# A recurrent loop's output products with tokens as weights, and its gates in halves by batch

## The reference

```
def step(carry, inp):
    w0_, w1_, w2_ = carry
    qi, ki, vi, lr0i, lr1i, lr2i = inp
    gate = ki @ w0_
    hb = ki @ w2_
    sg = silu(gate)
    hidden = sg * hb
    dhidden = vi @ w1_.transpose(0, 2, 1)
    dhbm = dhidden * sg
    dgate = dhidden * hb
    dgba = silu_backprop(dgate, gate)
    w1g = newtonschulz5(einsum('bch,bcd->bhd', hidden * lr1i, vi))
    w0g = newtonschulz5(einsum('bcd,bch->bdh', ki * lr0i, dgba))
    w2g = newtonschulz5(einsum('bcd,bch->bdh', ki * lr2i, dhbm))
    (each weight: w = w + wg, then its columns are scaled to their first norms)
    oi = silu(qi @ w0_) * (qi @ w2_) @ w1_
    return ((w0_, w1_, w2_), oi)
```

## Time and profile before

| | |
|---|---|
| runs | 1030.43, 1031.6, 1032.62 us, median 1031.6 |
| the profiled execution's span | 1028.6 us |
| PE / DVE / ACT / POOL busy | 970.8 / 702.0 / 564.1 / 435.5 us |
| recurrent loop | steps t = 1 to 7 from about 85 us to 363 us |
| granted TensorE clock | 0.998 of full speed over the span |

### The profile page before, as it was taken

One profiled execution on the slowest core, in us unless ns is written; L12 is line 12 of the kernel. 1 busy time (PEld: TensorE's weight loads), 2 busy tenths in 40 slices (PEclk: granted clock), 3 DMA queues, 4 the chain that ended last, 5 costly groups with the idle time before them and its releaser, 6 DMA issues.

```text
span 1028.6 us, 25039 instructions
## 1 busy us (share of the span) xinstructions
PE 970.8 (94%) x9714; PEld 737.7 (72%) x9714; DVE 702.0 (68%) x2121; ACT 564.1 (55%) x1450; POOL 435.5 (42%) x391
## 2 busy tenths in 40 slices
PE   5887999999999999999999999999999999999978
PEld 3566897887887755675656769786978687868546
DVE  4889988988989942213223676866686668776864
ACT  3667778777778732212223465555556556655541
POOL 1221240340541711101002666775677567779710
PEclk9999999999999999999999999999999999999999
DMA  9250000000000002900002321322132213211202
GB/s 313 68 195 2 2 0 0 0 0 0 0 2 2 2 1 48 308 1 0 1 1 51 84 61 44 72 63 52 43 73 63 52 43 72 58 37 45 92 2 84
DMA packets 32812, 52.36 MB, mean 51 GB/s; under 512 B 7760, under 2 KB 17744, under 8 KB 31824
## 3 DMA queue, kind: packets, MB, share of 16 engines
q1 hardware_dynamic: 32720, 51.10, 18.0%
HBM read 21.98 MB, written 2.10 MB: 23 GB/s over the span
## 4 chain that ended last, share of the span: by engine, by line
PE 54%; DVE 4%; ACT 2%; issue 1%
PE quad L2102 12%; PE quad L2061 10%; PE quad L1705 8%; PE quad L2119 7%; PE quad L2005 6%; PE quad L2133 5%; PE quad L2197 1%; PE quad L2069 1%; PE quad L1591 1%; ACT act_probs L2366 1%; PE quad L2024 1%; DVE act_probs L2457 1%; DVE wq_wo L2471 1%; DVE x_pairs L2487 0%; ACT act_probs L2357 0%
## 5 line engine op out<-in xcount | busy, mean ns | idle before, releaser
L2709 POOL TENSOR_TENSOR act_probs<-act_probs,rden 128x512 f32<-128x512 f32 (+3 forms) x128 | 169.0, 1327 | 111.1 <-DVE rden L2476 111.1
L2357 ACT ACTIVATE act_probs<-act_probs,neg_max 128x256 f32<-128x256 f32 (+3 forms) x256 | 140.9, 553 | 83.3 <-DVE neg_max L2457 83.1
L2061 PEld LDWEIGHTS quad<-hT,ug_queries 128*128 128x128 f32 x1024 | 122.6, 192 | 14.1 <-issue 7.7
L2061 PE MATMUL quad<-hT,ug_queries 128*128 128x128 f32 x1024 | 124.7, 275 | 0.8 <-DVE act_probs L1720 0.5
L2457 DVE CUSTOM_DVE_ANT_0 act_probs<-quad,mask 128x256 f32<-128x256 f32 (+3 forms) x256 | 115.1, 485 | 0.3 <-issue 0.3
L1705 PE MATMUL quad<-hT,ug_raw_switch 128*128 128x512 f32 x256 | 113.9, 595 | 0.0
L1720 DVE SCALAR_TENSOR_TENSOR act_probs<-quad,ws_up,silu_keys 128x512 f32<-128x512 f32 x32 | 24.0, 750 | 97.1 <-ACT silu_keys L1715 97.1
L1715 ACT ACTIVATE silu_keys<-quad,ws_gate 128x512 f32<-128x512 f32 x32 | 22.0, 687 | 118.7 <-PE quad L1705 118.7
L1705 PEld LDWEIGHTS quad<-hT,ug_raw_switch 128*128 128x128 f32 x256 | 47.5, 190 | 55.1 <-issue 54.3
L2476 DVE RECIPROCAL rden<-den 128x2 f32<-128x2 f32 x128 | 20.3, 159 | 94.2 <-ACT act_probs L2357 94.0
L2102 PE MATMUL quad<-down_raw_out,ug_raw_switch 128*128 128x256 f32 (+3 forms) x256 | 79.5, 438 | 3.6 <-DVE neg_max L2457 3.6
(11 more groups left out here) (330 smaller groups left out, 2285.7 us busy)
## 6 DMA issues: line engine op xcount, KB each, us to landing
rope_swapped<-gate SPq DMA_DIRECT2D x120, 64.0 KB, 2.0
ug_raw_switch<-gate SPq DMA_DIRECT2D x60, 128.0 KB, 2.3
ug_raw_switch<-in_wmod SPq DMA_DIRECT2D x4, 512.0 KB, 7.4
x_pairs<-in_x SPq DMA_DIRECT2D x4, 512.0 KB, 8.0
x_rows<-x_pairs SPq DMA_DIRECT2D x8, 256.0 KB, 5.0
wq_wo<-in_wq_nopeT SPq DMA_DIRECT2D x1, 2048.0 KB, 8.5
wq_wo<-in_wo SPq DMA_DIRECT2D x1, 2048.0 KB, 13.2
ug_queries<-in_switch_w SPq DMA_DIRECT2D x1, 2048.0 KB, 7.6
```

The lines of the kernel that those rows point to most:

```text
L2061: mm = nc.tensor.matmul(out[:, P * i:P * i + P], w[:, kt, HP * half + i, :], k.hT[:, kt, b, cols], start=(kt == 0), stop=(kt == KT - 1))
L2357: nc.scalar.activation(tile, tile, ACT.Exp, bias=neg_max[:, r, e:e + 1], scale=-1.0, accum_out=den[:, r, e:e + 1])\
L2709: nc.gpsimd.tensor_tensor(tile, tile, rden[:, t % RING, :].unsqueeze(2).to_broadcast([P, 2, cols]), ALU.mult)\
```

## The change

Two of the four output products of a step are formed for w0 and w2 at once: `out_gate(t, i)` has the 64 tokens of q as the stationary operand and 256 moving columns, as the gates have, so its result has tokens on the partitions, once for each pair. ACT takes the silu of half of bank 6 (`silu_gate`), DVE multiplies in place of `hidden_out` (`hidden_rows`), both once for each pair, and as the next product wants the hidden index on the partitions, `turn_hidden` transposes the four 128x128 blocks on PE and `take_hidden` copies them on ACT. The first pair's comes where `out_product(0, 0)` was, the second's where `out_product(1, 0)` was; the products in `early_out` and after (A, 1) are gone; the transposes stand before the turned v, and `out_rows` moves from behind (AA, 2) to behind (AA, 3). `silu_gate(t, 1)` stands ahead of the load of the Sqrt table. In place of `gates`, `gate(i, 1)` of both pairs comes first, waiting for weights 3 and 4 alone, then `gate(i, 0)` and `back(i)` of each pair; the gates lie in banks 4 and 3, `back` in banks 1 and 0. The first gradients wait for the four activations of the first pair. The tail after the loop keeps its `out_product`s. The constant for the output norm moves to the shared semaphore of constants.

```diff
-N_CONSTS = 4
+N_CONSTS = 5
...
-    PROJECT_V, TURN_OUT, TURN_V, TURN_QK, OUT_ROWS, SUMS, START = range(PH, PH + 7)
-    G_ORDER = ((GT, 0), (SUMS, 0), (OUT_ROWS, 0), (SUMS, 1), (SUMS, 2), (GT, 2), (SUMS, 3), (SUMS, 4), (GT, 4), (SUMS, 5))
+    PROJECT_V, TURN_OUT, TURN_V, TURN_QK, OUT_ROWS, SUMS, START, OUT_GATE, TURN_HID = range(PH, PH + 9)
+    GATE_BANK, DH_BANK = (4, 3), (1, 0)
+    G_ORDER = ((GT, 0), (SUMS, 0), (OUT_GATE, 1), (SUMS, 1), (SUMS, 2), (GT, 2), (SUMS, 3), (SUMS, 4), (GT, 4), (SUMS, 5))
     G_REST = (1, 3, 5)
-    INNER = ((A, 0), (A, 1), (OUT_ROWS, 1), (START, 0), (A, 2), (A, 3), (AA, 0), (A, 4), (AA, 1), (START, 1), (A, 5), (TURN_V, 0), (AA, 2), (OUT_ROWS, 0), (START, 2), (AA, 3), (Y, 0), (AA, 4), (AA, 5), (START, 3), (TURN_QK, 0), (Y, 1),
+    INNER = ((A, 0), (A, 1), (START, 0), (A, 2), (A, 3), (AA, 0), (A, 4), (AA, 1), (START, 1), (A, 5), (TURN_HID, 0), (TURN_V, 0), (AA, 2), (START, 2), (AA, 3), (OUT_ROWS, 0), (Y, 0), (AA, 4), (AA, 5), (START, 3), (TURN_QK, 0), (Y, 1),
...
-    TAKEN = ((AA, 0), (START, 0), (AA, 1), (TURN_V, 0), (START, 1), (AA, 2), (OUT_ROWS, 0), (START, 2), (TURN_QK, 0), (START, 3), (TURN_QK, 1), (TURN_OUT, 0), (START, 4), (A1, 0), (A1, 1), (A1, 2), (START, 5), (A1, 3), (A1, 4), (YT, 0), (A1, 5), (YT, 1), (TURN_OUT, 1), (YT, 2), (START, 6),
+    TAKEN = ((AA, 0), (START, 0), (AA, 1), (TURN_HID, 0), (TURN_V, 0), (START, 1), (AA, 2), (OUT_ROWS, 0), (START, 2), (TURN_QK, 0), (START, 3), (TURN_QK, 1), (TURN_OUT, 0), (START, 4), (A1, 0), (A1, 1), (A1, 2), (START, 5), (A1, 3), (A1, 4), (YT, 0), (A1, 5), (YT, 1), (TURN_OUT, 1), (YT, 2), (START, 6),
...
-            def gates(t):
-                for i in range(PAIRS):
-                    for hd in range(H):
-                        for j in range(2):
-                            mm = nc.tensor.matmul(bank[3 * i][C * j:C * j + C, 2 * HD * hd:2 * HD * hd + 2 * HD],
-                                                  kT[:, i, hd, C * j:C * j + C], weight[:, 3 * j:3 * j + 2, H * i + hd, :],
-                                                  start=True, stop=True)
+            def gate(i, j):
+                for hd in range(H):
+                    mm = nc.tensor.matmul(bank[GATE_BANK[i]][C * j:C * j + C, 2 * HD * hd:2 * HD * hd + 2 * HD],
+                                          kT[:, i, hd, C * j:C * j + C], weight[:, 3 * j:3 * j + 2, H * i + hd, :],
+                                          start=True, stop=True)
+                if j == 0:
                     mm.then_inc(s["gates_summed"], 1)
-                    for hd in range(H):
-                        for j in range(2):
-                            mm = nc.tensor.matmul(bank[3 * i + 1][C * j:C * j + C, HD * hd:HD * hd + HD],
-                                                  vT[:, i, hd, C * j:C * j + C], state[:, 3 * j + 2, H * i + hd, :],
-                                                  start=True, stop=True)
-                    mm.then_inc(s["gates_summed"], 1)
+
+            def back(i):
+                for hd in range(H):
+                    for j in range(2):
+                        mm = nc.tensor.matmul(bank[DH_BANK[i]][C * j:C * j + C, HD * hd:HD * hd + HD],
+                                              vT[:, i, hd, C * j:C * j + C], state[:, 3 * j + 2, H * i + hd, :],
+                                              start=True, stop=True)
+                mm.then_inc(s["gates_summed"], 1)
+
+            def out_gate(t, i):
+                if i == 0:
+                    pe.wait_ge(s["proj_taken"], t)
+                    pe.wait_ge(s["q_moved"], t)
+                else:
+                    pe.wait_ge(s["out_hidden"], 2 * t - 1)
+                for hd in range(H):
+                    for j in range(2):
+                        mm = nc.tensor.matmul(bank[6][C * j:C * j + C, 2 * HD * hd:2 * HD * hd + 2 * HD],
+                                              qT[:, i, hd, C * j:C * j + C], weight[:, 3 * j:3 * j + 2, H * i + hd, :],
+                                              start=True, stop=True)
+                mm.then_inc(s["out_summed"], 1)
+
+            def turn_hidden(t):
+                pe.wait_ge(s["out_hidden"], 2 * t)
+                for u in range(U):
+                    mm = nc.tensor.transpose(bank[6][:, P * u:P * u + P], h_o[:, P * u:P * u + P], k.eye[:])
+                mm.then_inc(s["o_turned"], 1)
...
             def out_rows(c, at=6):
-                pe.wait_ge(s["out_hidden"], c + 1)
+                if at == 6:
+                    pe.wait_ge(s["hid_taken"], c + 1)
+                else:
+                    pe.wait_ge(s["out_hidden"], 2 * NCH - 1)
...
-                def early_out(t):
-                    pe.wait_ge(s["proj_taken"], t)
-                    pe.wait_ge(s["q_moved"], t)
-                    begin(3, G)
-                    out_product(0, 1, 0)
-
...
-                if not first:
-                    early_out(t)
                 pe.wait_ge(s["qkv_taken"], 3 * (t + 1))
                 if first:
                     first_norm.wait_halves(pe, 3, 1)
                     pe.wait_ge(w_in, STATE_IN)
                 else:
-                    for q in (0, 1, 3, 4):
+                    for q in (3, 4):
                         begin(q, G)
-                    pe.wait_ge(s["w_scaled"], Q * t)
-                gates(t)
+                for i in range(PAIRS):
+                    gate(i, 1)
+                if not first:
+                    for q in (0, 1):
+                        begin(q, G)
+                for i in range(PAIRS):
+                    gate(i, 0)
+                    if i == 0 and not first:
+                        pe.wait_ge(s["w_scaled"], Q * t)
+                    back(i)
...
-                    begin(0, G)
-                    out_product(0, 0, 0)
+                    out_gate(t, 0)

                 pe.wait_ge(s["lr_applied"], PAIRS if first else 3 * PAIRS * (t + 1))
                 pe.wait_ge(s["dh_used"], 2 * PAIRS * (t + 1))
+                pe.wait_ge(s["gate_acted"], 4 * PAIRS * t + 4)
...
                     else:
-                        if n == 0:
-                            pe.wait_ge(s["out_silued"], t)
-                        out_product(1, n)
+                        out_gate(t, n)
...
+                    elif ph == TURN_HID and not first:
+                        turn_hidden(t)
                     elif ph == OUT_ROWS and not first:
-                        if n == 1:
-                            out_product(1, 1)
-                        else:
-                            out_rows(t - 1)
+                        out_rows(t - 1)
...
+            def silu_gate(t, i):
+                act.wait_ge(s["out_summed"], 2 * (t - 1) + i + 1)
+                nc.scalar.activation(h_o[:, H * P * i:H * P * i + H * P].rearrange("p (h d) -> p h d", h=H),
+                                     bank[6][:].rearrange("p (h g d) -> p h g d", h=H, g=2)[:, :, 0, :], ACT.Silu).then_inc(s["out_silued"], 1)
+
+            def take_hidden(t):
+                act.wait_ge(s["o_turned"], 2 * t - 1)
+                nc.scalar.activation(hid_o[:].rearrange("p i h c -> p (i h c)"), bank[6][:], ACT.Copy).then_inc(s["hid_taken"], 1)
+
...
-                act.wait_ge(s["o_turned"], c + 1)
+                act.wait_ge(s["o_turned"], 2 * c + 2 if at == 6 else 2 * c + 1)
...
-                gh = [bank[3 * i][:].rearrange("p (h g d) -> p h g d", h=H, g=2) for i in range(PAIRS)]
+                gh = [bank[GATE_BANK[i]][:].rearrange("p (h g d) -> p h g d", h=H, g=2) for i in range(PAIRS)]
...
                 if not first:
-                    silu_out(t - 1)
+                    silu_gate(t, 0)
                 for n, q in enumerate(MQ):
                     if n != G_DVE:
                         take(G, g_bf, q)
+                if not first:
+                    silu_gate(t, 1)
                 load_table(ACT.Sqrt)
...
+                    elif ph == TURN_HID and not first:
+                        take_hidden(t)
...
-            def hidden_out(c, at=6):
-                dve.wait_ge(s["out_silued"], c + 1)
+            def hidden_rows(t, i):
+                dve.wait_ge(s["out_silued"], 2 * (t - 1) + i + 1)
+                to = h_o[:, H * P * i:H * P * i + H * P].rearrange("p (h d) -> p h d", h=H)
+                nc.vector.tensor_tensor(to, bank[6][:].rearrange("p (h g d) -> p h g d", h=H, g=2)[:, :, 1, :], to, ALU.mult)\
+                    .then_inc(s["out_hidden"], 1)
+
+            def hidden_out(c, at):
+                dve.wait_ge(s["out_silued"], 2 * NCH - 1)
                 dve.wait_ge(s["out_summed"], 2 * c + 2)
                 nc.vector.tensor_tensor(hid_o[:].rearrange("p i h c -> p (i h c)"), bank[at][:], h_o[:], ALU.mult).then_inc(s["out_hidden"], 1)
...
-                dh = [bank[3 * i + 1][:, 0:D].rearrange("p (h d) -> p h d", h=H) for i in range(PAIRS)]
+                dh = [bank[DH_BANK[i]][:, 0:D].rearrange("p (h d) -> p h d", h=H) for i in range(PAIRS)]
...
                 by_silu(1)
```

(17 more changed lines are left out.)

## The result

The changed kernel takes 1040.1 us (median; 1038.4 to 1042.6) beside 1031.0 for the kernel before on the same chip (1029.3 to 1032.6): the ratio is 1.0083, with an interval of 1.0060 to 1.0105. It is slower, by about 9 us, where 7.0 were forecast. The profiled execution has a span of 1038.4 us where before has 1028.6.

A forecast was written before the change was run, and what follows sets the result against it. Each step was taken as a PE part, a mixed part and a DVE-bound part that any later start delays. 6 x 0.95 + 1.3 = 7.0 us; 1028.6 + 7.0 + 3.0 = 1038.6 us, range 1032.5 to 1041.5.

The forecast's parts named there:

- Gates in halves: PE up to the gradients: same-half instructions run in line, 15 x 0.216 = 3.24 us; stretch 4.30 against 3.78, +0.52.
- Rival 1: Gates: 64-wide instructions of one half overlap at 0.108 us each, a step ends 0.6 earlier, 1027.4 us; chance 0.08.
- Changes of width: PE switching between full-width and 64-wide instructions costs about 0.1 us each way; out_gate +0.13, so gradients start 0.65 later.
- Column sums: out_gate number 1 replaces the third output product on PE: 0.1 + 0.87 + 0.1 against 0.92, +0.15 us.
- ACT behind the table load: silu_gate number 1 ahead of the Sqrt table load uses up ACT's 0.32 us of room; 0 to 0.3 more.
- Rival 3: silu_gate ahead of the table load costs 0.3 us beyond the room each step; 1040.7 us; chance 0.14.
- Mixed part: First Newton-Schulz products: AA 4 instead of AA 3 holds DVE, 0.15 us later beyond the shift; bounds -0.5 to +0.3.
- Rival 2: Mixed part: out_rows behind AA 3 removes DVE's 0.73 us gap, giving back 0.5 a step; 1033.7 us; chance 0.18.
- the DVE part: Step from 224.10 to 244.60: DVE busy 20.32 of 20.50 us, so any later beginning lengthens the step by as much.
- Per step: Steps t = 1 to 6 each grow by 0.52 + 0.13 + 0.15 + 0.15 = 0.95 us.
- Last step: t = 7, without q/k norm on DVE: AA 4 comes 0.5 us later in place of 0.15, so 1.3 us in all.
- A step of 40 us, and 6.3 us to the gradient: Signs of being right: 40 us steps; last turned weight to first gradient 6.3 us where it was 5.65.

The follow-up runs named there:

- after_pool_held: The changed kernel with one wait more: in the last step POOL's copy of q waits for DVE's four normalisations; 1033.4 us, ratio 1.0021.
- before_pool_early: The kernel before with the last step's fourth output product moved up behind the third, releasing POOL early; 1038.0 us, ratio 1.0062.
- after_all_j1_then_j0: The changed kernel with POOL held in the last step, all weights awaited, then eight j = 1 gates, eight j = 0, then d_hidden; 1038.3 us, ratio 1.0077.

## Why the prediction was right in the whole and wrong in its parts

The direction held, and the time, 1040.1, is 1.5 above the forecast and inside its range. But that is luck: two errors of 4.1 and 4.8 us cancel. Of the 8.6 to 9.1 us that the runs show, 7.65 are there at the landmark behind the loop; the rest is put down to nothing here.

- **Gates in halves, +0.52 a step: wrong, -0.17.** The term "only the first of j = 0 runs beside the last of j = 1" failed. Four do, which is 0.65 us off the 4.30; 3.64 were measured. The pairs of rows 5 gave the right price of two in line and of two side by side; what they could not show is how far ahead a half is taken, and I put the lowest value into the sum. Rival 1 is out: instructions of one half stay 0.216 apart, not 0.108. What was gained came from the other half's starting early.
- **Changes of width, 0.1 each: right.** The transposes ahead of out_gate take 1.02 where 0.93 stood, and out_gate takes 1.01 with the change behind it (0.97 forecast). Together +0.16 where +0.13 stood. So the gradients, due 0.65 later, are 0.0 later.
- **Column sums, +0.15: right** (+0.17).
- **ACT behind the table load, 0 to 0.3, taken 0: a little low.** g_norm starts without any wait for PE, 0.55 behind g_total's product where it was 0.44 (217.16 to 217.71; 216.50 to 216.94): 0.11. Rival 3 is there in kind, with a third of its price. The turned gradients, which set the pace of the next products, come 0.17 later (218.15 - 0.49 against 217.49), so this 0.11 did not add to the column sums' 0.17.
- **Mixed part, +0.15: about right** (+0.08: 0.25 at the second polynomial, 0.17 at the column sums). The gap moved from AA 3 to AA 4 and is 1.11 where "about 1" was forecast. Rival 2, that DVE profits, is out, and the kernels with out_rows later say why: PE is as full as DVE there, and DVE's wait comes back ahead of a later product. That the DVE part is bound by DVE alone, as the first paragraph of the prediction has it, was too simple.
- **Per step:** 0.17 + 0.08 = 0.25 in the step of the rows; 0.29 between the mean steps of the table, 1.6 us for t = 1 to 6 by the landmark of the column sums, where 5.7 stood.
- **Last step, +1.3: wrong, 6.1** (7.65 at the landmark, less 1.6). Without the meeting (after_pool_held) the products do bring DVE to the state updates about 1 us late (352.92 against 351.01 before, of which 0.9 was there in the column sums), but at the next ones the two kernels are together again (357.77 and 357.62), and the last step is 0.5 us shorter than before's (44.33 and 44.83), so even the 1.3 went. The meeting puts 6.4 to 6.7 us on top. The prediction moved the second product ahead and looked only at those who wait for it in the loop. For the last step it counted PE and DVE; that POOL waits for both products before it moves q was not followed, though before's POOL row at 336.58 waits 8.79 us for PE. That is the step that failed: a released engine was costed at nothing, and it met DVE.
- **A step of 40 us, and 6.3 us to the gradient: wrong** (39.5, and 5.67). These two signs alone, read in the trace, would have told that the sum was right by luck.

What stays open: why an instruction starts up to four places ahead and no further, and what the 2.8 us at the lower clock cost by themselves in the last step; POOL's release was not tried without PE's pause.

## What to carry to other kernels

When a change moves a product earlier, list every engine that waits for its semaphore, in the first and last step too, and look what each does once released: an engine that starts earlier can slow another that it used to miss. Here 2.8 us earlier on an idle engine cost 6.4 us (before_pool_early). A wait that keeps such an engine off a short critical operation is cheap: one line gave back 6.4 of the 8.6 us. And where two engines are both full, moving work between places of one moves the other's wait and can make it longer; time the order, don't argue it from one gap.

## What the runs showed of the hardware that was not expected

- TensorE started 64-wide instructions ahead of others that stood before them in the program: L567 at 210.50 before L558 at 210.71 in after_all_j1_then_j0. By the spacing of the starts one column half passed three instructions of the other (206.697 and 206.703 in the changed kernel, 209.138 and 209.144 in after_all_j1_then_j0), while instructions of one half keep a distance of 0.216 us with 256 columns of f32. So halves don't have to alternate strictly here: of eight and eight, four still ran beside four.
- Four SBUF-to-SBUF operations of VectorE of 128x256 grew from 1.38 to 7.20 us beside GpSimd, each ending 0.15 us behind the end of a GpSimd operation of 1.26 to 2.40 us; four scalings of 128x512 took 4.66 us beside GpSimd and 2.50 alone.
- TensorE, idle from 338.17 to 344.60, was at a granted clock of 0.50 from 340.60 to 347.40, so for 2.8 us of its next work; in before_pool_early, idle from 337.62 to 344.23, from 342.09 to 348.92. With a pause of 0.35 us at this place (after_pool_held) it stayed at 1.00.
